# Zero-padding a bias product of 3 contraction rows to 128 in a graph network with a mixture of experts

## The chip, the cores and the metric

The kernel runs on one core of a Trainium2 chip. The metric is the device time of one execution in microseconds, as the median of several runs. The kernel before took 606.42 us in the median of three runs (605.57 to 607.59).

## The reference

There are 32 graphs of 256 tokens with 128 features each, 8192 tokens in all. The first half is a graph layer, the second a mixture of 8 experts:

```
agg = eps * xn + adj @ xn                      # xn = layernorm(x), per graph
h   = silu(rmsnorm(agg @ W1 + b1) * rms_w)     # 128 -> 512
x   = x + h @ W2 + b2                          # 512 -> 128
xn2 = layernorm(x); logits = xn2 @ router.T    # the two best of 8 experts
x   = x + sum over the two of gate * (silu(xn2 @ w1[e].T) * (xn2 @ w3[e].T)) @ w2[e].T
```

The two biases b1 (512 values) and b2 (128 values) are not zero, and rms_w is not one. The change touches how b1 and b2 are added.

## The kernel before, in words

The program has two large stages and a short end.

The **graph stage** is a pipeline over the 32 graphs, one step for each, `step(j)` with j from -4 to 35. A step works on several graphs at once, each at another phase. Each engine runs its own list of steps, and semaphores order them. Steps up to j = 7 and from j = 28 on are written out straight; steps 8 to 27 are a hardware loop of five rounds of four steps, where offsets and awaited counts come from registers.

TensorE's step (line 723) issues, in this order: `sum_neighbours(j+2)` (line 657, the product with the adjacency matrix, four matmuls), `second_product(j-1)` (lines 690 and 692: for each of the two halves of a graph, one bias product and eight matmuls with W2), `first_product(j+1)` (lines 677 to 680: for each half, one bias product and three matmuls with W1, which with its operand is split in a high and a low part), `transpose_rows(j-2)` (line 700), `transpose_hidden(j)` (line 665, eight), `rank(j-3)` (lines 719 and 720) and `router(j-2)` (line 709).

Both products start with their bias. The biases are cut in three bfloat16 parts whose sum is the float32 value, and these are the three rows of a tile `bias_cut` of 3 partitions by 640. A matmul of three rows of ones with these three rows puts the bias into every token's row of the PSUM bank, and the products accumulate on it. There are two of them for each of the two products, 4 in a step and 128 in the program. The tile is filled once at the start: VectorE cuts the bias (lines 954 to 962), SyncE writes the parts to a DRAM tensor and reads them back in the form of rows (lines 318 to 321), and TensorE waits for that (`s_biasrow`, line 748) before step -1.

ScalarE's step copies the high part of the neighbour sum (533), normalises (547), squares the hidden row for the RMS (556, twice), copies the transposed rows (562) and applies silu (540, twice). VectorE's step does the rest of the statistics (826, 891, 941 to 946), scales the hidden rows (833, twice), takes the low part of the neighbour sum (820), and does the routing (848 to 883). GpSimd's step raises spreads to the power -1/2 (445), adds epsilon to the adjacency's diagonal blocks (451), and from step 4 on sends the normalised rows of a graph to the lists of their experts with four indirect DMAs (458).

GpSimd also sets the constants at the start (lines 413 to 436). VectorE, ScalarE and TensorE wait for thirteen of these instructions (`s_const`). TensorE then runs matmuls without a use (`keep_busy`, line 742).

The **expert stage** goes over 71 tiles of 256 rows, each of one expert (lines 765 to 812). At the **end** the two results of each token are weighed and added. Neither has a bias product.

Of the kernel before, what the change touches and what calls it, by code (L numbers as in the profile page):

```python
# [19 lines left out]
BF16 = mybir.dt.bfloat16  # L20
# [6 lines left out]
P = 128  # L27
D = 128
# [5 lines left out]
H = 512  # L34
HC = H // P
BIAS = H + D
# [42 lines left out]
def positive(value):  # L79

    return not isinstance(value, int) or value > 0
# [13 lines left out]
def graph_moe_kernel(nc, x, adj_t, eps, w1, biases, rms_w, w2, router_t, ew13, ew2, out):  # L95
    ctx = ExitStack()
    with ctx:
        def sb(name, shape, dt=F32):
            return ctx.enter_context(nc.sbuf_tensor(name, shape, dt))
# [4 lines left out]
        def sem(name):  # L104
            return ctx.enter_context(nc.semaphore(name))
# [5 lines left out]
        bias_rows = nc.dram_tensor("bias_rows", (3, BIAS), BF16, kind="Internal").ap()  # L111
# [6 lines left out]
        ones = sb("ones", [P, P], BF16)  # L118
# [11 lines left out]
        bias_sb = sb("bias_sb", [P, BIAS // P])  # L130
        bias_rest = sb("bias_rest", [P, 2, BIAS // P])
        bias_part = sb("bias_part", [P, 3, BIAS // P], BF16)
        bias_cut = sb("bias_cut", [3, BIAS], BF16)

        tokens = sb("tokens", [P, TILES, D])
        adj = sb("adj", [P, 2, TT, N])
# [74 lines left out]
        hid_ps = [up_ps[0][:, (1 + t) * 512:(2 + t) * 512] for t in range(TT)]  # L211
        hidt_ps = [up_ps[1][:, t * 512:(t + 1) * 512] for t in range(TT)]
        y_ps = up_ps[1][:, 2 * 512:3 * 512]
# [12 lines left out]
        s_x = [sem(f"x_loaded{r}") for r in range(4)]  # L226
        s_adjin = [sem(f"adj_loaded{r}") for r in range(2)]
        s_mem = sem("constants_set"); s_const = sem("constants_ready")
        s_bcut = sem("bias_steps"); s_biasrow = sem("bias_rows_moved"); s_w1cut = sem("w1_split"); s_epsid = sem("eps_ident_ready")
        s_adj = sem("adj_ready"); s_st1 = sem("stats1_done"); s_st2 = sem("stats2_done"); s_mv = sem("mean_var_done")  # L230
        s_var = sem("var_ready"); s_inverse = sem("inverse_ready"); s_shift = sem("shift_ready"); s_normed = sem("normed_ready")
        s_agg = sem("agg_done"); s_agghi = sem("agg_hi_ready"); s_agglo = sem("agg_lo_ready")
# [27 lines left out]
        def run_expert_steps(eng, kind, ahead, step):  # L260

            def some(i, count):
                low = max(0, -ahead - i.off) if isinstance(i.k, int) else 0
                high = min(count, SLOT_TILES - ahead - i.off) if isinstance(i.k, int) else count
                experts = [None] * count
                if low < high:
                    _, experts[low:high] = nc.values_load_multi_w_load_instructions(
                        expert_int[0:1, bass.ds(i.plus(low + ahead).n, high - low)], engines=[kind], min_val=0,
                        max_val=E - 1, skip_runtime_bounds_check_because="sums of E - 1 comparisons")
                for q in range(count):  # L270
                    step(i.plus(q), experts[q])

            for j in range(X["first"], X["steady"], UNROLL):
                some(Step(0, j), UNROLL)
            with eng.Fori(0, X["bodies"]) as k:
                some(Step(k, X["steady"]), UNROLL)
            for j in range(X["steady"] + UNROLL * X["bodies"], X["last"] + 1, UNROLL):
                some(Step(0, j), min(UNROLL, X["last"] + 1 - j))
# [14 lines left out]
        def _(sp):  # L293
# [24 lines left out]
            sp.wait_ge(s_bcut, 5)  # L318
            sp.dma_start(bias_rows.rearrange("i (p f) -> p i f", p=P), bias_part[:, :, :]).then_inc(s_biasrow, 16)
            sp.wait_ge(s_biasrow, 16)  # L320
            sp.dma_start(bias_cut[:, :], bias_rows).then_inc(s_biasrow, 16)
            sp.dma_start(w2_sb[:, :, :], w2.rearrange("(c p) d -> p c d", p=P)).then_inc(s_w2, 16)
            load_step(Step(0, 2))
            load_step(Step(0, 3))
# [9 lines left out]
            for u in range(GRAPHS - UNROLL, GRAPHS):  # L334
# [5 lines left out]
                         padding[:, E:PADS, :, :]).then_inc(s_padded, 16)  # L340
            sp.wait_ge(s_cntint, 1)
            _, found = nc.values_load_multi_w_load_instructions(
                count_int[0:1, :], engines=[mybir.EngineType.SP], min_val=0, max_val=TOKENS,
                skip_runtime_bounds_check_because="an expert has at most one row of every token")
# [4 lines left out]
            def bases_of(i, count):  # L349
                _, bases = nc.values_load_multi_w_load_instructions(  # L350
                    base_int[0:1, bass.ds(i.n, count)], engines=[mybir.EngineType.SP], min_val=0,
                    max_val=E * CAP + (E - 2) * S,
                    skip_runtime_bounds_check_because="the list holds SLOT_TILES tiles, each within its region")
                return bases
# [56 lines left out]
        def _(pool):  # L411
# [2 lines left out]
            pool.memset(before[:, :], 1.0).then_inc(s_mem, 1)  # L414
            pool.memset(ones[:, :], 1.0).then_inc(s_const, 1)
            pool.memset(minus_half[:, :], -0.5).then_inc(s_const, 1)
            pool.wait_ge(s_mem, 2)
            pool.affine_select(out=ident[:, :], in_=ident[:, :], compare_op=ALU.not_equal, fill=1.0,
                               base=0, pattern=[[-1, P]], channel_multiplier=1).then_inc(s_const, 1)
# [228 lines left out]
        def _(pe):  # L648
# [20 lines left out]
            def first_product(u):  # L669
                r = u.ring(2)  # L670
                pe.wait_ge(s_agglo, u.plus(1).n)
                for t in range(TT):

                    if positive(u.n):
                        pe.wait_ge(s_scaled, u.n * TT + t - 1)
                    hi, lo = agg_hi[:, r, t * P:(t + 1) * P], agg_lo[:, r, t * P:(t + 1) * P]
                    pe.matmul(hid_ps[t][:, :], ones[0:3, :], bias_cut[:, 0:H], start=True, stop=False)  # L677
                    pe.matmul(hid_ps[t][:, :], lo, w1_hi[:, :], start=False, stop=False)  # L678
                    pe.matmul(hid_ps[t][:, :], hi, w1_lo[:, :], start=False, stop=False)  # L679
                    pe.matmul(hid_ps[t][:, :], hi, w1_hi[:, :], start=False, stop=True).then_inc(s_hid, 1)  # L680

            def second_product(u):
                pe.wait_ge(s_silu, u.n * TT + TT)

                if positive(u.n):
                    pe.wait_ge(s_x2, u.n)
                if positive(u.plus(-2).n):
                    pe.wait_ge(s_place, u.plus(-2).n)
                for t in range(TT):
                    pe.matmul(y_ps[:, t * D:(t + 1) * D], ones[0:3, :], bias_cut[:, H:H + D], start=True, stop=False)  # L690
                    for c in range(HC):
                        ins = pe.matmul(y_ps[:, t * D:(t + 1) * D], hidden_t[:, u.ring(2), t, c, :], w2_sb[:, c, :],  # L692
                                        start=False, stop=(c == HC - 1))
                ins.then_inc(s_y, 1)
# [28 lines left out]
            def step(j):  # L723
                if j.plus(2).within(GRAPHS):
                    sum_neighbours(j.plus(2))
                if j.plus(-1).within(GRAPHS):
                    second_product(j.plus(-1))
                if j.plus(1).within(GRAPHS):
                    first_product(j.plus(1))
                if j.plus(-2).within(GRAPHS):  # L730
                    transpose_rows(j.plus(-2))
                if j.within(GRAPHS):
                    transpose_hidden(j)
                if j.plus(-3).within(GRAPHS):
                    rank(j.plus(-3))
                if j.plus(-2).within(GRAPHS):
                    router(j.plus(-2))
# [392 lines left out]
```

## Time and profile before

| | |
|---|---|
| time, median of 3 runs | 606.42 us (605.57 to 607.59) |
| span of the profiled execution | 646.6 us |
| graph stage in the profile | 0 to about 309 us |
| expert stage | about 310 to 620 us |
| end | about 620 to 646.6 us |
| TensorE busy with matmuls | 544.2 us (84%) |
| GpSimd busy | 384.1 us (59%) |

The profiled execution's own time is not given beside its span; it is a single execution with every instruction recorded, and its span is 40.2 us longer than the median of the timed runs. In the profile PE is TensorE's matmuls and PEld its weight loads, DVE is VectorE, ACT is ScalarE, POOL is GpSimd and SP is SyncE. A line such as L677 is the line of the kernel that issued an instruction. In brackets stands how long the engine was idle before the instruction and what released it. The ends of matmuls are modelled, so that their starts are the times to go by.

### The profile page before, as it was taken

Reading aid. Unit: us, or ns where it says so; the run is one execution under the profiler, and the core shown is the slowest. Engines: PE = TensorE matmul, PEld = TensorE weight load, DVE = VectorE, ACT = ScalarE, POOL = GpSimd, SP = SyncE. Lnnn points to the kernel's source line nnn. Section 1 sums busy time; section 2 is a strip of 40 time slices with the busy share of each in tenths; the row PEclk is TensorE's granted clock in tenths of the full one; section 3 lists DMA queues with packets and bytes.
Section 4 is the critical chain, followed back from the end, with each engine's and each line's share of the span. In section 5 each row is a group of like instructions: output and inputs, shape, how many; then the busy total and the mean of one; then the engine's idle time right before and its main releaser. Section 6 shows DMA issues by size and latency. Waiting matters only on the chain.

```text
span 646.6 us, 13636 instructions
## 1 busy us (share of the span) xinstructions
PE 544.2 (84%) x3859; PEld 475.5 (74%) x3860; DVE 391.2 (60%) x1394; ACT 320.7 (50%) x701; POOL 384.1 (59%) x440
## 2 busy tenths in 40 slices
PE   6899989988999899995389999999999999897000
PEld 5567766666676666774389999999999999897000
DVE  3466664665566556665646666666666666464465
ACT  3366654455455555654145545545455455352343
POOL 5337765666576667667516777776777676577000
PEclk8699996899888989997679999999999999899555
DMA  5223321423232132311312222222222222121798
GB/s 140 64 73 108 120 85 50 125 73 102 72 109 85 57 122 74 108 35 42 117 56 69 69 76 70 77 69 65 82 66 78 69 65 72 59 68 44 218 312 254
DMA packets 66942, 59.76 MB, mean 92 GB/s; under 512 B 8407, under 2 KB 60890, under 8 KB 66918
## 3 DMA queue, kind: packets, MB, share of 16 engines
q1 hardware_dynamic: 57558, 41.10, 22.3%
q0 software_dynamic: 8640, 17.84, 8.3%
q10 hardware_dynamic: 720, 0.53, 0.3%
q8 instruction: 11, 0.18, 0.1%
q14 instruction: 13, 0.11, 0.1%
HBM read 35.42 MB, written 24.02 MB: 92 GB/s over the span
## 4 chain that ended last, share of the span: by engine, by line
PE 72%; DMA 6%; issue 5%; POOL 5%; ACT 4%; DVE 3%; another core or an unknown queue 2%; SPq 1%; DVEq 0%; POOLq 0%; ACTq 0%
PE route_ps L798 13%; PE up_ps L692 11%; PE up_ps L782 8%; PE up_ps L784 8%; PE up_ps L783 7%; PE up_ps L657 5%; PE up_ps L678 4%; DMA ew_sb<-results 3%; PE up_ps L677 3%; PE up_ps L680 3%; PE rowt_ps L769 2%; PE route_ps L709 2%; POOL expert_rows L458 2%; PE up_ps L679 2%
## 5 line engine op out<-in xcount | busy, mean ns | idle before, releaser
L507 POOL DMA_INDIRECT results<-result,dest x142 | 138.6, 976 | 34.9 <-issue 28.2
L458 POOL DMA_INDIRECT expert_rows<-rows,slot x128 | 125.9, 983 | 37.0 <-issue 34.2
L782 PE MATMUL up_ps<-rows_lo,up_hi 128*114 128x256 f32 x426 | 127.1, 298 | 3.8 <-DVE rows_lo L1032 3.8
L783 PE MATMUL up_ps<-rows_hi,up_lo 128*114 128x256 f32 x426 | 121.2, 285 | 0.0
L784 PE MATMUL up_ps<-rows_hi,up_hi 128*114 128x256 f32 x426 | 120.9, 284 | 0.0
L615 ACT ACTIVATE scaled<-up_ps 114x768 f32<-114x768 f32 x71 | 57.7, 813 | 116.6 <-PE up_ps L784 114.2
L798 PE MATMUL route_ps<-ew_sb,hidden_t 114*128 x852 | 106.8, 275 | 0.7 <-DVE result L1047 0.7
L798 PEld LDWEIGHTS route_ps<-ew_sb,hidden_t 114*128 114x128 f32 x852 | 100.7, 192 | 0.9 <-issue 0.9
L445 POOL TENSOR_TENSOR inverse<-spreads,minus_half 128x6 f32<-128x6 f32 (+2 forms) x37 | 46.0, 1243 | 70.3 <-DVE spreads L826 63.5
L1032 DVE TENSOR_TENSOR rows_lo<-rowt_ps,rows_hi 128x256 fp32r<-128x256 f32 x71 | 30.2, 425 | 92.5 <-ACT rows_hi L620 89.8
L692 PE MATMUL up_ps<-w_sb,hidden_t 128*128 128x128 f32 x512 | 82.1, 309 | 0.0
L496 POOL TENSOR_TENSOR dest<-slot_rows,zero_int 128x2 uint32<-128x2 uint32 x71 | 44.5, 626 | 62.1 <-DVE result L1047 42.8
L782 PEld LDWEIGHTS up_ps<-rows_lo,up_hi 128*114 128x114 f32 x426 | 76.6, 180 | 4.8 <-DVE rows_lo L1032 4.8
L556 ACT ACTIVATE squares<-up_ps 128x512 f32<-128x512 f32 x64 | 38.2, 598 | 82.8 <-PE up_ps L680 59.1
L784 PEld LDWEIGHTS up_ps<-rows_hi,up_hi 128*114 128x114 f32 x426 | 76.9, 181 | 0.0
L783 PEld LDWEIGHTS up_ps<-rows_hi,up_lo 128*114 128x114 f32 x426 | 76.9, 181 | 0.0
L692 PEld LDWEIGHTS up_ps<-w_sb,hidden_t 128*128 128x128 f32 x512 | 69.2, 210 | 4.7
L1040 DVE TENSOR_TENSOR hidden_t<-up_ps,scaled 114x768 f32<-114x768 f32 x71 | 67.3, 948 | 1.6 <-ACT scaled L615 1.6
L1025 DVE TENSOR_TENSOR up_lo<-ew_sb,up_hi 128x684 fp32r<-128x684 f32 x71 | 61.1, 861 | 1.4 <-issue 1.0
L608 ACT ACTIVATE up_hi<-ew_sb 128x684 fp32r x71 | 54.5, 768 | 7.3 <-issue 7.2
L833 DVE SCALAR_TENSOR_TENSOR scaled<-up_ps,inverse,rms_w_sb 128x512 f32<-128x512 f32 x64 | 44.7, 738 | 0.0
L657 PE MATMUL up_ps<-adj,normed 128*128 128x256 f32 x128 | 39.0, 431 | 3.6 <-DMA bias_cut<-bias_rows 3.2
(121 smaller groups left out, 888.5 us busy)
## 6 DMA issues: line engine op xcount, KB each, us to landing
slot_rows<-expert_rows SPq DMA_DIRECT2D x71, 130.0 KB
adj<-in_adj_t SPq DMA_DIRECT2D x32, 256.0 KB
ew_sb<-results SPq DMA_DIRECT2D x32, 256.0 KB, 4.0
tokens<-in_x SPq DMA_DIRECT2D x32, 128.0 KB
out<-tokens SPq DMA_DIRECT2D x16, 256.0 KB, 3.6
ew_sb<-in_ew SPq DMA_DIRECT2D x6, 456.0 KB
results<-result,dest POOLq DMA_INDIRECT x142
expert_rows<-rows,slot POOLq DMA_INDIRECT x128
```

The lines of the kernel that those rows point to most:

```text
L458: pool.indirect_dma_start(out=expert_rows, out_offset=bass.IndirectOffsetOnAxis(ap=slot[:, r, n:n + 1], axis=0), in_=rows[:, r, n // TT, n ...
L507: pool.indirect_dma_start(out=results, out_offset=bass.IndirectOffsetOnAxis(ap=dest[:, r, h:h + 1], axis=0), in_=result[:, r, h, :], in_of ...
L608: act.activation(up_hi[:, i.ring(2), :], ew13_sb[:, bass.ds(expert * (2 * EHP), 2 * EHP)], ACT.Copy).then_inc(s_uphi, 1)
L615: act.activation(silu1[:, r, :], h1_ps[r], ACT.Silu).then_inc(s_silu1, 1)
L657: ins = pe.matmul(agg_ps[:, 0:N], normed[:, r, c, :], adj[:, r, c, :], start=(c == 0), stop=(c == TT - 1))
L692: ins = pe.matmul(y_ps[:, t * D:(t + 1) * D], hidden_t[:, u.ring(2), t, c, :], w2_sb[:, c, :], start=False, stop=(c == HC - 1))
L782: pe.matmul(part, up_hi[:, r, at], rows_lo[:, r, :], start=True, stop=False)
L783: pe.matmul(part, up_lo[:, r, at], rows_hi[:, r, :], start=False, stop=False)
L784: ins = pe.matmul(part, up_hi[:, r, at], rows_hi[:, r, :], start=False, stop=True)
L798: ins = pe.matmul(result_ps[:, h * D:(h + 1) * D], prod[:, r, c * S + h * P:c * S + (h + 1) * P], ew2_sb[:, bass.ds((expert * CHUNKS + c) ...
L1025: dve.tensor_tensor(up_lo[:, r, :], ew13_sb[:, bass.ds(expert * (2 * EHP), 2 * EHP)], up_hi[:, r, :].bitcast(F32), ALU.subtract)
L1040: dve.tensor_tensor(prod[:, r, :], h3_ps[r], silu1[:, r, :], ALU.mult).then_inc(s_prod, 1)
```

## The change

The tile of bias rows gets 128 partitions. GpSimd sets all of it to zero at the start, SyncE's read-back writes rows 0 to 2 and waits for the zeroing first, and the two bias products contract over all 128 partitions of `ones` and of the tile; 125 of the products' rows are zero.

```diff
-        bias_cut = sb("bias_cut", [3, BIAS], BF16)
+        bias_cut = sb("bias_cut", [P, BIAS], BF16)
...
+        s_biaszero = sem("bias_cut_cleared")
...
             sp.wait_ge(s_biasrow, 16)
-            sp.dma_start(bias_cut[:, :], bias_rows).then_inc(s_biasrow, 16)
+            sp.wait_ge(s_biaszero, 1)
+            sp.dma_start(bias_cut[0:3, :], bias_rows).then_inc(s_biasrow, 16)
...
             pool.memset(minus_half[:, :], -0.5).then_inc(s_const, 1)
+            pool.memset(bias_cut[:, :], 0.0).then_inc(s_biaszero, 1)
...
-                    pe.matmul(hid_ps[t][:, :], ones[0:3, :], bias_cut[:, 0:H], start=True, stop=False)
+                    pe.matmul(hid_ps[t][:, :], ones[:, :], bias_cut[:, 0:H], start=True, stop=False)
...
-                    pe.matmul(y_ps[:, t * D:(t + 1) * D], ones[0:3, :], bias_cut[:, H:H + D], start=True, stop=False)
+                    pe.matmul(y_ps[:, t * D:(t + 1) * D], ones[:, :], bias_cut[:, H:H + D], start=True, stop=False)
```

## Rows read from the trace of the kernel before

**Rows 1.** Windows: each engine's busy us (instructions), granted clock, DMA share, GB/s.

```profile
45.00:75.00 30.00, 30.00 (x193) 22.74 (x192) 21.65 (x124) 19.99 (x52) 20.39 (x22) 1.00 0.33 104
205.70:214.70 9.00, 7.62 (x50) 5.73 (x49) 5.47 (x31) 4.94 (x14) 5.96 (x7) 1.00 0.25 73
100.20:112.20 12.00, 12.00 (x50) 8.91 (x49) 5.58 (x31) 5.36 (x14) 6.66 (x7) 0.57 0.20 56
```

**Rows 2.** Timeline of PE (start us, us, what): steps written straight, one with its products.

```profile
50.90 1.11 PE L657 MATMUL up_ps<-adj,normed 128*128 128x256 f32 x4
...
60.73 0.23 PE L690 MATMUL up_ps<-bias_cut,ones 3*128 3x128 bf16 x1
...
61.98 0.38 PE L677 MATMUL up_ps<-bias_cut,ones 3*128 3x512 bf16 x1
62.29 0.50 PE L678 MATMUL up_ps<-w_hi,agg_lo 128*128 128x512 f32 x1
62.63 0.39 PE L679 MATMUL up_ps<-w_lo,agg_hi 128*128 128x512 f32 x1
62.85 0.39 PE L680 MATMUL up_ps<-w_hi,agg_hi 128*128 128x512 f32 x1
63.18 0.39 PE L677 MATMUL up_ps<-bias_cut,ones 3*128 3x512 bf16 x1
...
64.51 1.04 PE L665 MATMUL up_ps<-ident,scaled 128*128 128x128 f32 x8
65.38 0.17 PE L719 MATMUL up_ps<-mask,before 128*128 128x8 bf16 x1
...
73.56 1.11 PE L657 MATMUL up_ps<-adj,normed 128*128 128x256 f32 x4
```

**Rows 3.** Timeline of PEld: weight loads of L678, L679 and, a step later, L719.

```profile
62.29 0.19 PEld L678 LDWEIGHTS up_ps<-w_hi,agg_lo 128*128 128x128 f32 x1 [0.23 <-issue]
62.40 0.19 PEld L679 LDWEIGHTS up_ps<-w_lo,agg_hi 128*128 128x128 f32 x1
...
72.86 0.10 PEld L719 LDWEIGHTS up_ps<-mask,before 128*128 128x128 bf16 x1
```

**Rows 4.** Timeline of PE: L719's matmul after the last of those loads.

```profile
72.97 0.17 PE L719 MATMUL up_ps<-mask,before 128*128 128x8 bf16 x1
```

**Rows 5.** Timeline of POOL: a first and a later straight step, a loop step, the tail.

```profile
50.45 1.33 POOL L445 TENSOR_TENSOR inverse<-spreads,minus_half 128x6 f32<-128x6 f32 x1 [4.97 <-DVE spreads L826]
...
58.01 1.35 POOL L445 TENSOR_TENSOR inverse<-spreads,minus_half 128x6 f32<-128x6 f32 x1 [0.31 <-issue]
...
177.61 1.36 POOL L445 TENSOR_TENSOR inverse<-spreads,minus_half 128x6 f32<-128x6 f32 x1 [1.86 <-DVE spreads L826]
...
183.80 0.96 POOL L458 DMA_INDIRECT expert_rows<-rows,slot  x1 [0.30 <-issue]
...
282.12 1.05 POOL L445 TENSOR_TENSOR inverse<-spreads,minus_half 128x4 f32<-128x4 f32 x1 [1.15 <-DVE spreads L826]
```

**Rows 6.** Timeline of a loop step: PE's last product, and ACT's square of it.

```profile
174.63 0.40 PE L680 MATMUL up_ps<-w_hi,agg_hi 128*128 128x512 f32 x1
...
176.63 0.60 ACT L556 ACTIVATE squares<-up_ps 128x512 f32<-128x512 f32 x1 [2.00 <-remote]
```

**Rows 7.** Timeline of DVE: its last work before a first product can start.

```profile
68.96 0.41 DVE L820 TENSOR_TENSOR agg_lo<-up_ps,agg_hi 128x256 fp32r<-128x256 f32 x1
```

**Rows 8.** Timeline at the start, of PE, POOL, DVE and SP.

```profile
12.86 2.05 PE L657 MATMUL up_ps<-adj,normed 128*128 128x256 f32 x4 [3.23 <-DMA bias_cut<-bias_rows]
...
2.88 0.53 POOL L481 MEMSET padding<- 128x520 f32 x1
...
3.61 0.49 DVE L901 BATCH_NORM_STATS2 stats<-tokens 128x6 f32<-128x128 f32 x2 [3.49 <-DMA tokens<-in_x]
...
9.32 0.33 SPq L321 DMA_DIRECT2D bias_cut<-bias_rows  x1
```

More of the change, by code:

```diff
@@ L228, in graph_moe_kernel @@
         s_mem = sem("constants_set"); s_const = sem("constants_ready")
-        s_bcut = sem("bias_steps"); s_biasrow = sem("bias_rows_moved"); s_w1cut = sem("w1_split"); s_epsid = sem("eps_ident_ready")
+        s_bcut = sem("bias_steps"); s_biasrow = sem("bias_rows_moved"); s_biaszero = sem("bias_cut_cleared"); s_w1cut = sem("w1_split"); s_epsid = sem("eps_ident_ready")
         s_adj = sem("adj_ready"); s_st1 = sem("stats1_done"); s_st2 = sem("stats2_done"); s_mv = sem("mean_var_done")
```

## The prediction

> **What bounds the kernel now.** I read the windows first. In the steps written straight TensorE is busy for all of 30.00 us at full clock [rows 1], and its steps take (73.56 - 50.90) / 3 = 7.55 us [rows 2]. In the loop a step takes 9.0 us, with TensorE busy for 7.62 and the clock still at 1.00 [rows 1]: there it waits.
>
> The timelines say for what. In step 17 TensorE's last product starts at 174.63 and lasts 0.40, so that it ends at 175.03; ScalarE's square of it starts only at 176.63, after 2.00 us of idling that the profile puts down to no engine [rows 6]. GpSimd then starts at 177.61 [rows 5]. Something holds back TensorE's signal for 1.6 us. I take this for something that the recording of every instruction brings with it: twenty loop steps that are 9.05 - 7.55 = 1.5 us too long make 30 us, and the profiled span is 646.6 - 606.42 = 40.2 us longer than the median. So the sum is made with steps of 7.55 us throughout, and set against the 606.42; the profile alone can't prove it.
>
> Next I read GpSimd. From 177.61 to the end of its fourth send (183.80 + 0.96 = 184.76) a full step takes it 7.15 us; the shortest gap before the next one is 0.31 [rows 5]. Its floor is thus 7.46 us a step, 0.09 below TensorE's 7.55. These two are nearly level from step 4 on. Before step 4 GpSimd has no sends, and idles for 4.97 us before its work at 50.45 [rows 5]: there TensorE alone is the limit.
>
> **What the change removes: two exposed weight loads at each bias product.** In a first product the starts are 61.98, 62.29, 62.63, 62.85, 63.18 [rows 2]. Between two matmuls of 128 rows (L679 to L680) it is 0.22; I use 0.23. The three that touch the 3-row product (into it, out of it, and the one after it, whose own load is late) take 0.33, 0.31 and 0.34. The weight loads show why: L679's load starts at 62.40, 0.23 before its matmul at 62.63, beside the matmul ahead. L678's load starts at 62.29, with its matmul and after 0.23 of idling: nothing is loaded ahead across a 3-row product [rows 3]. A 128-row product in bfloat16 among float32 ones does get its load ahead: L719's starts at 72.86, its matmul at 72.97 [rows 3, 4].
>
> With 128 rows I expect four even matmuls: 4 x 0.23 = 0.92 in place of 63.18 - 61.98 = 1.20, so 0.28 less. In a second product half the nine matmuls take 61.98 - 60.73 = 1.25; eight transposes of the same 128 columns take 65.38 - 64.51 = 0.87, or 0.109 each, and nine of these 0.98: 0.27 less [rows 2]. A step has two of each: 2 x 0.28 + 2 x 0.27 = 1.10 us less on TensorE, 6.45 in place of 7.55. Bounds for this: nothing at all, if the loads are late for another reason, and 1.10.
>
> The Trainium skill bears on both. TensorEngine Tiling, Key Properties, states that a change of the tiling mode drains TensorE. By that rule a 3-row product among 128-row ones pays twice, and the change ends it; the trace agrees, with the 0.23 of idling before L678's load. TensorE: Matmul & The Clock Gate, under The mechanism (Part 3), says that a weight load overlaps matmuls in flight only where its row group differs. By that rule a 128-row bias load would still be exposed and the sum would be 0; the trace disagrees, since L679's load of 128 rows goes out 0.23 ahead of its matmul.
>
> **What it adds.** Streaming is by columns, which stay 512 and 128. The zeroing is one instruction on GpSimd, 640 bfloat16 on each of 128 partitions; the nearest row, 520 float32 on 128, took 0.53 [rows 8]. So it costs between 0 and 0.53, and I take 0.4, as the bytes are fewer. It stands before the constants that VectorE, ScalarE and TensorE wait for. VectorE is covered: it starts at 3.61, held by the tokens' DMA, well after the constants (GpSimd begins the next thing, the padding, at 2.88). TensorE's useless matmuls start up to 0.4 later, but at step -1 it idles for 3.23 us for the bias rows' DMA [rows 8], which takes that up. SyncE's new wait stands before the read-back at 9.32 [rows 8], when the zeroing is some 7 us old; behind it are queued W2 and the next adjacency and token loads, and nothing of them moves. The DMA writes the same three rows. All this is 0; without that cover it would be 0.4.
>
> **The sum.**
> - Steps -1 and 0, four first products on the path: 4 x 0.28 = 1.1, and at the half clock of the start up to double, 2.2. I take 1.6.
> - Steps 1 to 3, TensorE alone: 3 x 1.10 = 3.3.
> - Steps 4 to 28, 25 of them, until GpSimd is the bound: 25 x 0.09 = 2.3. The other 1.0 of each turns into idle time of TensorE.
> - The tail, steps 29 and 30: GpSimd has idled for 1.15 us there at 282.12 [rows 5] and has less to do, so that I give 0.8 and 0.4, together 1.2 (bounds 0 and 2.2).
> - Expert stage and end: no bias product, 0.
>
> Together 8.4 us, so 606.4 - 8.4 = 598.0. This case's own range is 595 to 602: the upper end without the terms of GpSimd and the tail, or with only one of the two loads of each product won; the lower with the upper bounds of start and tail and a GpSimd floor that is 0.05 a step lower.
>
> **The rivals.**
>
> *More, because GpSimd is no floor in the timed runs.* Its 7.15 comes from a recorded execution, and its gaps of 0.30 between sends could be the recording's. The next floor is the chain from one first product to the next through ScalarE, GpSimd and VectorE. Its last link, the low part of the neighbour sum, ends at 68.96 + 0.41 = 69.37 [rows 7]; the bias product then comes at about 61.98 + 7.55 = 69.53. With 0.16 of slack and 0.56 less in the two first products a step can't go below 7.55 - 0.16 - 0.56 = 6.83. That gives 25 x 0.72 = 18.0 for steps 4 to 28, and 1.6 + 3.3 + 1.2 with it: 24.1, or 582. Against it: the send is GpSimd's own work, and 7.46 shows in straight and loop steps alike.
>
> *Much more, because the held signals are real.* If loop steps take 9.05 in the timed runs too, TensorE's signal comes 1.1 us sooner, perhaps ahead of the hold, and up to 20 x 1.5 = 30 us go: 570. The difference of 40.2 us between span and median speaks against it.
>
> *It doesn't do what it says.* The load is late because the type changes from bfloat16 to float32, not for its rows. No row shows a float32 load after a bfloat16 product without a wait, so this is open, though L719 shows the other direction. Then nothing changes: 606.4.
>
> *Slower: the clock.* TensorE goes from no idle time in a step to 7.46 - 6.45 = 1.0 us in each. The straight steps, without idling, keep the clock at 1.00 throughout. The loop steps idle for 1.4, and some of them lose the clock: the one in 100.20:112.20 has 0.57 on average between the two levels of 2.4 and 1.2 GHz, and lasts 12.00 in place of 9.0, 3.0 more [rows 1]. The place is steps 4 to 28 and the price 3.0 for each such step. Three of them eat the 8.4; from four on the kernel is slower by over 0.3%; with one step in three, 8 of 25, it is 24 - 8.4 = 15.6 slower, 622. For it: the idle share would be 13%, close to the loop's 16%. Against it: most loop steps keep the full clock, and shorter losses fit into the idle time. A milder form, two or three such steps, ends at 606.
>
> **How the numbers follow.** Forecast 0.46; GpSimd no floor 0.17; held signals real 0.05; no effect 0.15; clock, mild 0.05; clock, hard 0.12. A change below 0.3% (1.8 us) can't be told from none. Faster by more: 0.46 + 0.17 + 0.05 = 0.68. Within: 0.15 + 0.05 = 0.20. Slower: 0.12. The range must reach to 582, the first rival, and to 608, past no effect; it leaves out the held signals, the hard clock and a bit of the first rival's lower part, some 0.2. The predicted time is 598.0.
>
> **What would show it.** In the changed kernel's profile the bias product's form reads 128*128 128x512; the weight loads of L678 and of both bias products start ahead of their matmuls; starts within a first product are 0.23 apart and the tile's pitch is 0.92; the straight steps 1 to 3 take about 6.45; from step 4 GpSimd's starts of its power are 7.4 to 7.5 apart with gaps of 0.3 while TensorE shows some 1.0 of waiting. The mean granted clock should stay near that of before. The recorded span may drop by more than the timed runs if the held signals are dodged. I am wrong if the pitch stays at 1.20 (no effect), if it is 0.92 and steps fall towards 6.8 (no floor), or if windows of 0.6 to 0.8 clock become common in steps 4 to 28.

## The result, and the profile after

The changed kernel took 585.66 us in the median of four runs (583.62 to 588.57); the kernel before, on the same chip, 607.0 us (605.57 to 608.57). The ratio is 0.9662, with a 95% interval of 0.963 to 0.9694. The change takes 21.3 us away, where 8.4 were forecast. The time lies inside the range given (582 to 608), far below the 598.0, and below that case's own range of 595 to 602. The range reached that low only for the sake of a rival that turned out false, so that the time lies in it by luck.

The profiled execution of the changed kernel has a span of 582.9 us and took 584.63 us itself. The kernel before was profiled a second time (the first experiment below): span 607.4 us, its own time 609.43. That is an execution like the timed ones, which the first recording of 646.6 us was not, and from here on it stands for the kernel before. The two spans differ by 24.5 us. The execution of before was 3.4 us above its own median, so some 3 us of the 24.5 are variation between executions.

**TensorE in a step.** The timeline of PE in the changed kernel, in step 3, answers to [rows 2] (start us, us, what). Line numbers are 2 higher than before from GpSimd's part on.

```profile
33.94 1.11 PE L659 MATMUL up_ps<-adj,normed 128*128 128x256 f32 x4
34.88 0.22 PE L692 MATMUL up_ps<-bias_cut,ones 128*128 128x128 bf16 x1
34.94 1.11 PE L694 MATMUL up_ps<-w_sb,hidden_t 128*128 128x128 f32 x8
35.88 0.22 PE L692 MATMUL up_ps<-bias_cut,ones 128*128 128x128 bf16 x1
35.94 1.11 PE L694 MATMUL up_ps<-w_sb,hidden_t 128*128 128x128 f32 x8
36.89 0.38 PE L679 MATMUL up_ps<-bias_cut,ones 128*128 128x512 bf16 x1
36.91 0.58 PE L680 MATMUL up_ps<-w_hi,agg_lo 128*128 128x512 f32 x1
37.34 0.40 PE L681 MATMUL up_ps<-w_lo,agg_hi 128*128 128x512 f32 x1
37.57 0.40 PE L682 MATMUL up_ps<-w_hi,agg_hi 128*128 128x512 f32 x1
37.81 0.39 PE L679 MATMUL up_ps<-bias_cut,ones 128*128 128x512 bf16 x1
...
40.41 0.46 PE L659 MATMUL up_ps<-adj,normed 128*128 128x256 f32 x1
```

From one first-product half to the next it is 37.81 - 36.89 = 0.92 us, from one second-product half to the next 35.88 - 34.88 = 1.00, and the step takes 40.41 - 33.94 = 6.47. The forecast had 0.92, 0.98 and 6.45.

Within the half the starts aren't the even 0.23 that were forecast: they are 0.02, 0.43, 0.23 and 0.24 apart. The weight loads (PEld) of the same stretch show that not every load goes ahead of its matmul, either:

```profile
36.89 0.19 PEld L680 LDWEIGHTS up_ps<-w_hi,agg_lo 128*128 128x128 f32 x1
37.10 0.19 PEld L681 LDWEIGHTS up_ps<-w_lo,agg_hi 128*128 128x128 f32 x1
...
37.80 0.10 PEld L679 LDWEIGHTS up_ps<-bias_cut,ones 128*128 128x128 bf16 x1 [0.28 <-issue]
```

L681's load starts 0.24 ahead of its matmul at 37.34, but L680's load starts only 0.02 ahead of its matmul at 36.91, and the second bias load 0.01 ahead of its own at 37.81. The half is 0.28 shorter all the same.

**GpSimd.** Its timeline in the changed kernel, over a whole loop step, answers to [rows 5]; in brackets stands the idle time ahead.

```profile
153.44 1.36 POOL L447 TENSOR_TENSOR inverse<-spreads,minus_half 128x6 f32<-128x6 f32 x1
154.79 0.72 POOL L453 TENSOR_TENSOR adj<-adj,eps_ident 128x256 f32<-128x256 f32 x1
155.68 1.03 POOL L460 DMA_INDIRECT expert_rows<-rows,slot  x1 [0.18 <-issue]
157.02 0.95 POOL L460 DMA_INDIRECT expert_rows<-rows,slot  x1 [0.30 <-issue]
158.28 0.96 POOL L460 DMA_INDIRECT expert_rows<-rows,slot  x1 [0.30 <-issue]
159.55 0.96 POOL L460 DMA_INDIRECT expert_rows<-rows,slot  x1 [0.30 <-DVE spreads L948]
160.53 1.35 POOL L447 TENSOR_TENSOR inverse<-spreads,minus_half 128x6 f32<-128x6 f32 x1
```

The power now starts 0.02 us after the end of the last send. The period is 160.53 - 153.44 = 7.09 us, not 7.4 to 7.5. The gap of 0.31 ahead of the power is gone.

**The stretch of the loop.** Windows of both kernels over the same stretch, first the second profile of before, then the changed kernel. Columns are the window, its length, the busy us (instructions) of PE, PEld, DVE, ACT and POOL, the granted clock, DMA share and GB/s.

```profile
80.00:225.00 145.00, 144.71 (x919) 109.96 (x918) 107.04 (x594) 94.77 (x249) 114.76 (x115) 1.00 0.34 106
```

```profile
80.00:225.00 145.00, 138.37 (x994) 118.73 (x993) 126.03 (x638) 99.09 (x267) 121.87 (x124) 1.00 0.37 111
```

TensorE was idle for 0.3 us of the 145 before, and now for 6.6; the clock stays at 1.00 (2.4 GHz) in both. What the engines wait for in the changed kernel in this stretch (two rows of the list; us in total, times, longest us):

```profile
...
PEld up_ps L679 <- DVE scaled L835: 13.2, 35, 0.6
...
DVE shift L893 <- POOL inverse L447: 2.5, 6, 0.6
```

Read from below it can be a chain: GpSimd's power releases VectorE, VectorE scales the hidden rows, and the first product waits for a PSUM bank that this frees. The lower row is small, so the rows alone don't prove that GpSimd sets the pace; the experiments with less epsilon below do.

**Where the 24.5 us come from.** The first matmul of `sum_neighbours` marks each step of TensorE (32 of them, steps -2 to 29). Here stand those of steps 1, 4 and 29 and the last matmul of the graph stage, of the second profile of before and then of the changed kernel.

```profile
28.23 1.03 PE L657 MATMUL up_ps<-adj,normed 128*128 128x256 f32 x4
49.98 1.11 PE L657 MATMUL up_ps<-adj,normed 128*128 128x256 f32 x4
239.16 1.11 PE L657 MATMUL up_ps<-adj,normed 128*128 128x256 f32 x4
271.91 0.17 PE L756 MATMUL rowt_ps<-taken,ones 128*128 128x8 bf16 x1
```

```profile
21.28 1.03 PE L659 MATMUL up_ps<-adj,normed 128*128 128x256 f32 x4
40.41 1.11 PE L659 MATMUL up_ps<-adj,normed 128*128 128x256 f32 x4
216.51 1.11 PE L659 MATMUL up_ps<-adj,normed 128*128 128x256 f32 x4
247.37 0.17 PE L758 MATMUL rowt_ps<-taken,ones 128*128 128x8 bf16 x1
```

| part | before | after | difference | forecast |
|---|---|---|---|---|
| up to step 1 | 28.23 | 21.28 | 6.95 | 1.6 |
| steps 1 to 3 | 21.75 | 19.13 | 2.6 | 3.3 |
| steps 4 to 28 (25) | 189.18 (7.57 each) | 176.10 (7.04 each) | 13.1 | 2.3 |
| step 29 to the end of the stage | 32.75 | 30.86 | 1.9 | 1.2 |
| sum | 271.91 | 247.37 | 24.5 | 8.4 |

The sum is the whole difference of the spans, so the later stages gave nothing. Two terms were far off: steps 4 to 28, and the start. Between the medians the difference is 21.3; if the variation between executions sits in the start, which these runs don't prove, the start is worth 21.3 - 2.6 - 13.1 - 1.9 = 3.7.

### The profile page after: what moved, and what is told of

The parts are those of the page before. It is cut to its first block, busy times and chain, and to the rows that moved or that the text cites. A ratio compares the mean times of both kernels' runs of the same rounds, so it can differ in the third digit from the quotient of the medians.

```text
span 582.9 us, 13638 instructions
## 1 busy us (share of the span) xinstructions
PE 493.5 (85%) x3859; PEld 460.1 (79%) x3860; DVE 405.6 (70%) x1394; ACT 317.0 (54%) x701; POOL 383.2 (66%) x441
## 4 chain that ended last, share of the span: by engine, by line
PE 61%; DVE 11%; POOL 10%; issue 8%; DMA 7%; SPq 2%; DVEq 1%; ACT 0%; POOLq 0%
PE route_ps L800 15%; PE up_ps L784 9%; PE up_ps L785 8%; PE up_ps L786 8%; POOL expert_rows L460 5%; DMA ew_sb<-results 4%; DVE scaled L835 3%; PE up_ps L667 3%; PE rowt_ps L771 3%; POOL inverse L447 2%; PE up_ps L679 2%; PE up_ps L694 2%; PE up_ps L682 2%; PE up_ps L680 2%; DVE chosen L885 2%
## 5 line engine op out<-in xcount | busy, mean ns | idle before, releaser
L694 PE MATMUL up_ps<-w_sb,hidden_t 128*128 128x128 f32 x512 | 67.6, 282 | 0.0
L694 PEld LDWEIGHTS up_ps<-w_sb,hidden_t 128*128 128x128 f32 x512 | 62.2, 192 | 3.6
L549 ACT ACTIVATE rows<-tokens,shift,inverse 128x128 f32 (+1 forms) x64 | 28.1, 486 | 42.2 <-DVE shift L893 42.2
```

## The experiments

Step times below are those of steps 4 to 28, worked out as in the table. All times are medians, "before" is the kernel before on the same chip, and a ratio stands with its 95% interval.

### The kernel before, once more

No edit. Is the loop step 9.05 us [rows 1, 6], or 7.55?

> The kernel before, unchanged. Recorded once at 646.6 us, timed at 607.0. Theory (the first recording was an untypical execution, in which TensorE's signals were held back in the loop steps): a second recording has a span near 605, loop steps of 7.5 to 7.6 us in place of 9.05, and the squares of line 556 start within 0.1 us of the end of the matmul they wait for. Rival (recording itself costs 40 us, or the hold is in every execution): the span is again near 646 and loop steps again take 9.0.

It took 605.98 us (ratio 1.0007, 0.9977 to 1.0037), and its profile shows steps of 7.57 us with no idle time on TensorE in the loop (the first windows row above). The held-back signals of [rows 6] aren't there. The long steps of the loop belonged to one untypical execution; what made it so stays open, since it didn't come again. The sum was rightly made with 7.55.

What matters more is GpSimd's row in this profile:

```profile
154.09 0.95 POOL L458 DMA_INDIRECT expert_rows<-rows,slot  x1 [0.30 <-issue]
155.37 1.35 POOL L445 TENSOR_TENSOR inverse<-spreads,minus_half 128x6 f32<-128x6 f32 x1 [0.32 <-DVE spreads L826]
```

The gap ahead of the power is here 0.32, and its releaser is VectorE, not "issue" as in [rows 5].

### One product alone

```diff
 first only
-  pe.matmul(y_ps[...], ones[:, :], bias_cut[:, H:H + D], start=True, stop=False)
+  pe.matmul(y_ps[...], ones[0:3, :], bias_cut[0:3, H:H + D], start=True, stop=False)
 second only
-  pe.matmul(hid_ps[t][:, :], ones[:, :], bias_cut[:, 0:H], start=True, stop=False)
+  pe.matmul(hid_ps[t][:, :], ones[0:3, :], bias_cut[0:3, 0:H], start=True, stop=False)
```

> Only the first product's bias contracts over 128 rows; the second product's stays at 3 rows. Theory (each bias product among 128-row matmuls costs an exposed load on each side; from step 4 on GpSimd's 7.05 us a step is the floor, which is what the changed kernel shows): TensorE's step falls from 7.55 by 0.56 to 6.99, still at or under GpSimd's floor, so nearly all of the gain of 21.3 us stays, about 17 to 20 us: 587 to 590. Rival (the gain is made in proportion to TensorE's time in every step, with no floor in between): half of it, 596.

> Only the second product's bias contracts over 128 rows. Same theory: TensorE's step falls by 0.54 to 7.01, again about GpSimd's floor: 587 to 591. If e1 and e2 both keep over 80% of the gain, the two halves don't add, and another engine is the floor; if each keeps half, they add and TensorE alone sets the step.

First only took 588.33 us (0.9698, 0.9639 to 0.9758), second only 592.58 (0.977, 0.9711 to 0.9829). Steps take 7.05 and 7.11 us. Either edit alone takes TensorE from 7.55 to about 7.0, which is where GpSimd stands: both together give 7.04. In these two kernels TensorE is still busy for 144.53 and 144.66 of the 145 us of the stretch, so that it and GpSimd are about level. So the two gains (18 and 14 us) don't add up to the 21, and half of what the change saves on TensorE is already beyond the floor. The second's 14 are 65% of the gain, and its time lies above the 587 to 591 that were forecast. The lead of the first over the second lies mostly at the start: its profile reaches step 1 at 22.76 us, that of the second at 28.41, as before.

### The added parts alone

```diff
-  pe.matmul(..., ones[:, :], bias_cut[:, ...], start=True, stop=False)
+  pe.matmul(..., ones[0:3, :], bias_cut[0:3, ...], start=True, stop=False)
```

This is done in both products; the tile keeps its 128 partitions and its zeroing.

> The tile has 128 partitions, GpSimd zeroes it and SyncE waits for that, but both bias products contract over 3 rows as before. Theory (what the change adds is covered): 607, within 1 us of the kernel before. Rival (the gain comes from the start, through another order of the constants): faster by more than 2 us.

606.03 us (0.999, 0.9964 to 1.0016): the zeroing, the larger tile and SyncE's wait cost nothing that can be measured. The forecast's size of the zeroing was too low, though its cover holds. GpSimd at the start of the changed kernel:

```profile
1.23 0.64 POOL L418 MEMSET bias_cut<- 128x640 bf16 x1
```

It took 0.64 us, above the 0.53 that I had set as its upper bound [rows 8]: between these two rows the time goes with the columns (520 and 640) and not with the bytes.

### Rows: 64 or 65 in place of 128

```diff
-  pe.matmul(..., ones[:, :], bias_cut[:, ...], start=True, stop=False)
+  pe.matmul(..., ones[0:64, :], bias_cut[0:64, ...], start=True, stop=False)
```

The same with 0:65 in the second kernel.

```diff
+  pe.matmul(..., ones[0:65, :], bias_cut[0:65, ...], start=True, stop=False)
```

> The tile is zeroed and has 128 partitions as in the changed kernel, but both bias products contract over 64 rows. Theory (what costs is that a product uses the array in another partition of its rows than its neighbours, so that their loads can't go ahead): 64 rows are still such another partition, the loads stay exposed, a tile's pitch stays at 1.20 us and the time at 606. Rival (the cost is of having very few rows, or shrinks with the rows): the pitch lies between 0.92 and 1.20 and the time between 586 and 606.

> As e4, but over 65 rows, one more. Theory: more than 64 rows take the whole array like the neighbours' 128, the loads go ahead, the pitch is 0.92 and the time that of the changed kernel, 586. Rival (the cost falls evenly with the rows, or vanishes only at 128): same time as e4 within 1 us.

With 64 rows 606.71 us (1.0007, 0.9982 to 1.0032), with 65 rows 584.95 (0.9651, 0.9615 to 0.9687). One row decides over all of it. The timelines of PE, first with 64 rows:

```profile
155.28 0.39 PE L679 MATMUL up_ps<-bias_cut,ones 64*128 64x512 bf16 x1
155.60 0.50 PE L680 MATMUL up_ps<-w_hi,agg_lo 128*128 128x512 f32 x1
...
156.50 0.39 PE L679 MATMUL up_ps<-bias_cut,ones 64*128 64x512 bf16 x1
```

```profile
151.28 0.39 PE L679 MATMUL up_ps<-bias_cut,ones 65*128 65x512 bf16 x1 [0.33 <-DVE scaled L835]
151.31 0.58 PE L680 MATMUL up_ps<-w_hi,agg_lo 128*128 128x512 f32 x1
...
152.20 0.39 PE L679 MATMUL up_ps<-bias_cut,ones 65*128 65x512 bf16 x1
```

With 64 rows the half takes 1.22 us, with 65 rows 0.92. In the weight loads of the 64-row kernel the load after the bias product comes only with its matmul, 0.32 after the bias product's start and after idling, as in [rows 3]; with 65 rows the next matmul starts 0.03 after the bias product:

```profile
155.60 0.19 PEld L680 LDWEIGHTS up_ps<-w_hi,agg_lo 128*128 128x128 f32 x1 [0.23 <-issue]
```

The types and columns are the same in both kernels. So the rival "it is the type, not the rows" is false, and so would be "the more rows, the better". A product of 3 or of 64 rows among 128-row ones pays, one of 65 or of 128 doesn't.

### The bias products side by side

Three rows, as before; the first product's two bias products stand together, so that TensorE goes from 128 rows to 3 and back once instead of twice.

```diff
   for t in range(TT):
-      hi, lo = agg_hi[...], agg_lo[...]
       pe.matmul(hid_ps[t][:, :], ones[0:3, :], bias_cut[:, 0:H], start=True, stop=False)
+  for t in range(TT):
+      hi, lo = agg_hi[...], agg_lo[...]
       ...   (the three matmuls)
```

> The kernel before with its 3-row products, but the first product's two bias products (of the two halves) are issued next to each other, ahead of the six others; the second product's stay where they are. Theory (the cost comes with each change between 3 rows and 128 rows, not with the 3-row product): one pair of changes less in a step, 0.28 us, steps of 7.27, and over 28 steps 8 us less: 598 to 599. Rival (each 3-row product costs, wherever it stands): 606.

599.03 us (0.9875, 0.9846 to 0.9904 against 606.82 of before): 7.8 us less, with steps of 7.29 in place of 7.57. That is one of the four 0.28 of a step. The weight loads show that the two of 3 rows go out together and only the load behind them idles:

```profile
153.03 0.11 PEld L676 LDWEIGHTS up_ps<-bias_cut,ones 3*128 3x128 bf16 x2
153.56 0.19 PEld L679 LDWEIGHTS up_ps<-w_hi,agg_lo 128*128 128x128 f32 x1 [0.42 <-issue]
```

The price is thus for each change to few rows and back, not for each small product. The Trainium skill, TensorEngine Tiling (Array Packing), Key Properties, says that a change of the tiling mode drains TensorE; the 0.28 for each change agrees with it. That a plain matmul of 3 or of 64 rows counts as such a change is only inferred, from the runs with 64 and 65 rows.

### Is GpSimd the floor?

GpSimd adds epsilon on only 8 of 128 columns of each diagonal block. Epsilon is left out elsewhere, so part of the computation is missing. (Epsilon is 0 in the inputs of all runs here.)

```diff
-  pool.tensor_tensor(blocks, blocks, eps_ident ..., ALU.add)
+  pool.tensor_tensor(blocks[:, :, 0:8], blocks[:, :, 0:8], eps_ident[:, 0:8] ..., ALU.add)
```

Once in the changed kernel and once in the kernel before:

> The changed kernel, with GpSimd's adding of epsilon to the adjacency's diagonal blocks cut to 8 of 128 columns (left out for the others; epsilon is 0 in these inputs). It takes some 0.5 us off each of GpSimd's steps. Theory (from step 4 on GpSimd is the floor of the changed kernel at 7.05 a step): steps fall to about 6.8, where the chain through ScalarE, GpSimd and VectorE is next, 25 x 0.25 = 6 us: 579 to 581. Rival (VectorE or that chain is already the floor): no change, 586. Second rival (nothing but TensorE is behind GpSimd): steps of 6.5, 573.

> The same cut of GpSimd's work, in the kernel before. Theory (TensorE alone sets its steps of 7.55): 606, no change. Rival (GpSimd and TensorE are both near the limit, and GpSimd's part shows as well): faster by 3 us or more.

The changed kernel goes to 571.64 us (0.9416, 0.9395 to 0.9437), 14 us below the full change, and the kernel before stays at 605.72 (0.9981, 0.9963 to 0.9999). The same 0.5 us of GpSimd in each step is worth 14 us in the one and about 1 in the other: before, TensorE alone was the bound, after, GpSimd is. The 14 are more than the 5 to 7 that were forecast; the time is close to the 573 of the rival with nothing but TensorE behind GpSimd. Steps written straight now take 6.48 us and all 25 take 6.54 in the mean. That is nearly TensorE's own time again. The windows row:

```profile
80.00:225.00 145.00, 142.06 (x1046) 124.54 (x1055) 117.57 (x675) 105.52 (x278) 119.92 (x132) 1.00 0.37 114
```

The floor of 6.83 that I had worked out for the chain from one first product to the next isn't there, since the steps go 0.3 below it.

### Where the epsilon is added

Three forms that have the whole of the reference's epsilon, on top of the change. In the first TensorE adds epsilon, by two more matmuls into the neighbour sum; in the second VectorE takes one of the two blocks; in the third VectorE takes both. In the first and the third GpSimd keeps an addition of one column.

```diff
 by TensorE:
+  pe.matmul(agg_ps[:, c * P:(c + 1) * P], normed[:, r, c, :], eps_ident[:, :], start=False, stop=(c == TT - 1))
 half by VectorE:
   pool: block = adj[:, u.ring(2), 0, 0:P]
+  dve:  block = adj[:, v.ring(2), 1, P:2 * P]   (at the end of VectorE's step)
 all by VectorE:
+  dve.tensor_tensor(blocks, blocks, eps_ident ..., ALU.add)   (in place of GpSimd's)
```

> The changed kernel, with epsilon's part of the neighbour sum as two more float32 matmuls of TensorE (with eps times the identity), in place of GpSimd's addition to the adjacency; GpSimd keeps a one-column instruction in its place. Theory (GpSimd's 7.05 is the floor, TensorE at 6.49 is next): GpSimd falls to 6.5, TensorE rises by 4 passes of 0.109, 0.44, to 6.93, and is the bound: 25 x 0.12 = 3 us less, 583. Rival (float32 matmuls of this kind cost more on the path, as their result ends the neighbour sum): no change or slower, 586 to 590.

> The changed kernel, with one of the two diagonal blocks' epsilon added by VectorE at the end of its step and one by GpSimd. Theory: GpSimd's step falls by about 0.36 to 6.70, VectorE's work rises from 6.13 by 0.25 to 6.4, TensorE stays at 6.49: steps of 6.7, 25 x 0.35 = 9 us less: 577. Rival (VectorE, busy for 87% of a step in the changed kernel, is as near to the limit as GpSimd): 583 to 588.

> The changed kernel, with both blocks' epsilon added by VectorE. GpSimd falls to about 6.5, VectorE rises by 0.4 to 6.55 of work, TensorE stays at 6.49. Theory (the largest of the three sums is the floor): steps of 6.55 to 6.7, 574 to 577. Rival (VectorE's waits inside its step come on top, some 0.3): steps of 6.85 or more, 581 or slower, and slower than e10.

| kernel | median us | ratio (95%) | step |
|---|---|---|---|
| by TensorE | 583.63 | 0.9617 (0.9593 to 0.9641) | 6.96 |
| half by VectorE | 579.92 | 0.9559 (0.9533 to 0.9584) | 6.82 |
| all by VectorE | 576.48 | 0.9504 (0.9477 to 0.953) | 6.68 |

By TensorE and all by VectorE took what was forecast (583, and 574 to 577); half by VectorE was forecast at 577 with steps of 6.70 and missed that by 3 us. By TensorE the bound changes over to TensorE: it is busy for 144.31 of the 145 us of the stretch, at 6.96 a step, and little is won. The less GpSimd has to do, the shorter the step, until GpSimd and TensorE are nearly level. GpSimd in the last kernel:

```profile
149.14 1.36 POOL L448 TENSOR_TENSOR inverse<-spreads,minus_half 128x6 f32<-128x6 f32 x1
150.49 0.18 POOL L470 TENSOR_TENSOR spacer<-minus_half 128x1 f32<-128x1 f32 x1
...
154.70 1.19 POOL L454 DMA_INDIRECT expert_rows<-rows,slot  x1 [0.31 <-issue]
155.91 1.36 POOL L448 TENSOR_TENSOR inverse<-spreads,minus_half 128x6 f32<-128x6 f32 x1
```

It still works without a pause, at 6.77 for this step; one send here took 1.19 us in place of 0.96. What lengthened it wasn't tested; VectorE's addition of 256 columns ran beside it, at 154.63. This kernel is the fastest of those that compute everything: 9 us below the changed kernel and 30 below the one before.

## Why the prediction was wrong in its size

**Right: the price of the 3 rows.** Four changes to 3 rows and back a step, 1.10 us in all, was the forecast; where TensorE is the bound, the step went from 7.55 to 6.48, 1.07 less. That it is the rows was shown by 64 against 65, and that it is the change to few rows and back, by the bias products side by side. A bias product of 128 rows in bfloat16 doesn't bring the stall. The rival "no effect" is false. That the price is two weight loads that can't go ahead is shown less well: the forecast sign, that the loads of L678 and of both bias products start ahead of their matmuls, came about for one bias load (36.78, matmul 36.89) and not for the other or for the load behind the bias product, and yet 0.28 were saved. What TensorE does in the 0.28 stays open.

**Right: the unusual recording.** The long loop steps were not those of the timed runs. The rival "held signals real" is false.

**Wrong: "until GpSimd is the bound: 25 x 0.09 = 2.3".** This is the step that failed. The bound was the right engine at the wrong level. I took GpSimd's floor as 7.15 + 0.31 = 7.46, because the shortest gap that I saw ahead of its power was 0.31 and the row put it down to "issue". But a gap that stays while another engine sets the pace shows what the engine waited for as much as what it needs. The profiles settle it: the releaser of that gap in the second profile of before is VectorE, the changed kernel has 0.02 in its place, and the floor is 7.04 to 7.09. The work from the power to the end of the last send, too, is 159.55 + 0.96 - 153.44 = 7.07 there and not 7.15. The term is then 25 x (7.55 - 7.06) = 12.3; measured 13.1. With it the same sum comes to 8.4 - 2.3 + 12.3 = 18.4.

**Wrong: the start, 1.6.** The durations at half clock were read as they stood in the profile, and I asked only how much shorter the products become. What changed most was the clock itself. Here are the windows of the start, of the second profile of before and then of the changed kernel:

```profile
8.00:18.00 10.00, 6.64 (x17) 3.57 (x17) 3.25 (x14) 2.98 (x8) 3.22 (x6) 0.65 0.39 105
18.00:28.00 10.00, 7.78 (x21) 4.79 (x20) 3.48 (x11) 3.64 (x10) 2.64 (x4) 0.50 0.13 39
```

```profile
8.00:18.00 10.00, 4.63 (x20) 3.07 (x18) 4.32 (x17) 4.19 (x12) 5.80 (x9) 1.00 0.46 135
18.00:28.00 10.00, 9.41 (x58) 7.51 (x58) 6.65 (x24) 6.44 (x17) 3.15 (x5) 1.00 0.18 53
```

Right after the wait for the bias rows the same four matmuls take twice as long in the one as in the other, though TensorE idled for 3.36 us ahead of them in the first and 2.87 in the second:

```profile
12.32 2.05 PE L657 MATMUL up_ps<-adj,normed 128*128 128x256 f32 x4 [3.36 <-DMA bias_cut<-bias_rows]
```

```profile
11.70 1.10 PE L659 MATMUL up_ps<-adj,normed 128*128 128x256 f32 x4 [2.87 <-DMA bias_cut<-bias_rows]
```

This difference can't come from the bias products: the first of them starts only behind these four matmuls, at 14.30 and 12.64 us. Other profiles have it the other way round, first the kernel with 65 rows, then before with less epsilon:

```profile
12.17 2.04 PE L659 MATMUL up_ps<-adj,normed 128*128 128x256 f32 x4 [2.42 <-DMA bias_cut<-bias_rows]
```

```profile
12.22 1.10 PE L657 MATMUL up_ps<-adj,normed 128*128 128x256 f32 x4 [2.81 <-DMA bias_cut<-bias_rows]
```

The first of these reached step 1 at 23.40 us, the second at 26.58. So with the four matmuls slow in both kernels the start differs by 28.23 - 23.40 = 4.8 us, with them fast in both by 26.58 - 21.28 = 5.3, and about 2 of the 6.95 came from how the clock happened to stand before any bias product.

After them it looks different. In the second stretch TensorE is at its lower level, 1.2 GHz, before, and at 2.4 GHz after. Over the profiles this goes with the rows of the first product: the kernels with 3 rows there (the two profiles of before, the added parts alone, second only, side by side, and before with less epsilon) have 0.50 to 0.67 in 18 to 28 us, while those with 64 rows or more have 0.83 or 1.00. But the kernel with 64 rows reached step 1 at 23.87 us, in an execution of 604.25, and was no faster than before in the median, and each of these is one execution. The kernel before varies as well: its timed executions went from 601.84 us, with a mean granted clock of 0.938, to 610.84, with 0.921, and none of the quickest was profiled. Why the clock stays up is open, and so is how often it does.

**The rivals on the clock** didn't come about: the granted clock is 1.00 over 145 us. But TensorE idled there for only 6.6 us in some 20 steps, 0.3 in each and not the 1.0 of their condition, so that what 1.0 would do wasn't tested.

**The rival "GpSimd is no floor"** gave 582, close to what was measured, by the wrong way. GpSimd is the floor (14 us more went when 0.5 us of its work did), and the chain of 6.83 is no bound. That the number was close is chance.

## What to carry to other kernels

Count the contraction rows of every small matmul against those of its neighbours: here a product of 3 rows among 128-row ones cost 0.28 us beyond its streaming, and one of 64 as much, zero rows up to 65 or more take that away, and small products side by side pay it once together. When an engine is relieved, take the floor of the next one from its own instructions, and count a gap at its end into the floor only if it is there too when nobody else sets the pace; the test is to cut some of that engine's work in both kernels. And if two engines are nearly level, a second edit on the relieved one is worth little until the other is relieved too: here the first of the two edits alone had 18 of the 21 us.

## What the runs showed of the hardware

- The step between 64 and 65 contraction rows: 606.71 against 584.95 us for the same kernel.
- Across a bias product of 65 rows or more the float32 matmul behind it starts only 0.02 to 0.04 us after the bfloat16 one and lasts 0.58, while starts over the whole half stay 0.92 apart. The ends are modelled, so that the time over the whole half should be read.
- One recording of a kernel can be far from its timed runs: 646.6 us once, 607.4 the next time, with loop steps of 8.4 to 12.0 us in the first and 7.57 in the mean in the second.
